# A four-layer transformer on one core: who normalises the MLP's rows, and how semaphores are cleared

## The reference, cut to what matters

```
for i in range(DEPTH):                      # 4
    y = layernorm(h, ln1_w[i], ln1_b[i])
    ...                                     # 8-head attention
    h = h + (o @ proj_w[i] + proj_b[i])
    y = layernorm(h, ln2_w[i], ln2_b[i])
    y = gelu(y @ fc1_w[i] + fc1_b[i])       # 128 -> 256
    h = h + (y @ fc2_w[i] + fc2_b[i])       # 256 -> 128
```

## Time and profile before

| | |
|---|---|
| time, median of 3 runs | 3908.1 us (3902.67 to 3911.08) |
| profiled execution, its own time | 3896.24 us |
| its span | 3894.5 us |
| granted TensorE clock, mean over the span | 0.95 of full speed |
| busy: PE, DVE, ACT, POOL | 3477.2, 2445.2, 1919.0, 2285.7 us |
| DVE L805, multiply by rstd | 128 times, 0.68 us |
| ACT L600, copy of `M2` | 128 times, 0.50 us |
| POOL L98, clears | 244 |

### The profile page before, as it was taken

How to read it: one execution, slowest core, us unless ns; L and a number is a source line. 1 busy time by engine, 2 the same in 40 slices (tenths; PEclk the granted TensorE clock), 3 DMA queues, 4 the chain that set the end, 5 groups by cost and what they waited for, 6 DMA issues and landing times. The chain is left out here.

```text
span 3894.5 us, 89214 instructions
## 1 busy us (share of the span) xinstructions
PE 3477.2 (89%) x30012; PEld 2650.4 (68%) x30012; DVE 2445.2 (63%) x6227; ACT 1919.0 (49%) x3500; POOL 2285.7 (59%) x2633
## 2 busy tenths in 40 slices
PE   6999999889999989999988999996997888989883
PEld 4567777667877767777666787775444666657662
DVE  2167776657777646777665777766995887743110
ACT  0156666436666535666643666653563433213331
POOL 0256663666665475666365666545994663463876
PEclk9999999989999989999998999998998999989986
DMA  6856663146776025666313667600111223232432
GB/s 220 246 103 129 128 130 74 20 76 122 132 128 131 11 57 99 131 128 129 74 20 74 128 129 131 129 2 26 35 32 29 63 63 45 54 82 45 70 58 29
DMA packets 456054, 342.05 MB, mean 88 GB/s; under 512 B 70659, under 2 KB 440171, under 8 KB 455595
## 3 DMA queue, kind: packets, MB, share of 16 engines
q1 hardware_dynamic: 404419, 275.69, 36.2%
q10 hardware_dynamic: 24224, 46.44, 3.7%
q0 software_dynamic: 27136, 16.42, 3.2%
HBM read 227.69 MB, written 109.29 MB: 87 GB/s over the span
## 5 line engine op out<-in xcount | busy, mean ns | idle before, releaser
L730 DVE TENSOR_REDUCE a_neg_max<-a_S 99x4 f32<-99x788 f32 x1024 | 1003.3, 980 | 491.1 <-PE a_S L319 486.8
L528 ACT ACTIVATE a_shared<-a_St 99x792 f32<-99x792 f32 (+1 forms) x1024 | 850.3, 830 | 614.2 <-PE a_St L336 602.7
L319 PE MATMUL a_S<-a_k_st,a_q_st 96*99 96x197 bf16 x4096 | 545.8, 256 | 47.0 <-DVE a_neg_max L730 46.8
L319 PEld LDWEIGHTS a_S<-a_k_st,a_q_st 96*99 96x99 bf16 x4096 | 394.4, 127 | 265.0 <-DVE a_neg_max L730 228.9
L336 PE MATMUL a_St<-a_q_st,a_k_st 99*99 99x198 bf16 (+1 forms) x4096 | 523.3, 250 | 43.0 <-DMA a_q_st<-a_max_rows 28.0
L355 PE MATMUL a_O<-a_shared,a_v_aug 99*32 99x198 f32 (+1 forms) x8192 | 461.8, 338 | 0.4
L336 PEld LDWEIGHTS a_St<-a_q_st,a_k_st 99*99 99x99 bf16 (+1 forms) x4096 | 385.8, 125 | 72.8 <-DMA a_q_st<-a_max_rows 32.8
L355 PEld LDWEIGHTS a_O<-a_shared,a_v_aug 99*32 99x32 f32 (+1 forms) x8192 | 246.2, 110 | 82.9 <-ACT a_shared L528 1.0
L659 POOL CAST a_parts<-a_q_k 128x792 bf16<-128x792 f32 x128 | 107.8, 843 | 311.1 <-issue 260.3
L673 POOL TENSOR_TENSOR h<-h,a_rows 99x512 f32<-99x512 f32 x128 | 163.2, 1275 | 212.4 <-DVE a_shared L805 212.4
L641 POOL CAST a_max_parts<-a_neg_max 99x32 bf16<-99x32 f32 x128 | 26.8, 209 | 440.7 <-DVE a_neg_max L730 440.7
(11 more groups left out here) (265 smaller groups left out, 7517.3 us busy)
## 6 DMA issues: line engine op xcount, KB each, us to landing
a_shared<-in_x ACTq DMA_DIRECT2D x64, 594.0 KB, 5.0
spill_q<-a_parts SPq DMA_DIRECT2D x384, 99.0 KB
spill_k<-a_parts SPq DMA_DIRECT2D x384, 99.0 KB
a_k_st<-spill_k SPq DMA_DIRECT2D x128, 297.0 KB
a_q_st<-spill_q SPq DMA_DIRECT2D x128, 297.0 KB
a_k_st<-spill_k SPq DMA_DIRECT2D x128, 198.0 KB
a_q_st<-spill_q SPq DMA_DIRECT2D x128, 198.0 KB
a_k_st<-spill_k SPq DMA_DIRECT2D x128, 99.0 KB
```

What stands on the lines that cost most here:

```text
L319: mm = nc.tensor.matmul(S[0:TC, j // 2, j % 2 * TB:j % 2 * TB + NTOK], q_st[p % 4][0:SPLIT, head, b * TB + c * TC:b * TB + (c + 1) * TC], ...
L528: nc.scalar.activation(probs[0:keys, u % 4, :].rearrange("p (x t) -> p x t", x=2), St[0:keys, :, 0:2 * TB], ACT.Exp).then_inc(s["probs"], 1)
L730: nc.vector.tensor_reduce(out.rearrange("p (x y) -> p x y", x=2), S[0:TC, :, 0:2 * TB].rearrange("p x (y t) -> p x y t", y=2)[:, :, :, 0:N ...
```

## The change

ACT, not DVE, multiplies the MLP's rows by rstd: four instructions of 128 columns in place of one of 512, for pair k+3 in turn k (before: pair k+2). DVE, not ACT, copies `M2` to `m_yT`, between the statistics and the addition to `h`. The statistics on DVE and the rstd on POOL are those of pair k+4, so one more filling turn, `mlp(l, -4)`, stands after step 30. POOL's bias stays with pair k+2. And `Sems.clear` issues one clear for each run of neighbouring semaphore numbers.

```diff
     def clear(self):
-        for s in self.all.values():
-            self.nc.gpsimd.sem_clear(s)
+        nums = sorted(s.num for s in self.all.values())
+        first = nums[0]
+        for a, b in zip(nums, nums[1:] + [None]):
+            if b != a + 1:
+                self.nc.gpsimd.sem_clear(range(first, a + 1))
+                first = b
         self.nc.all_engine_barrier()
...
                     step(l, PAIRS - 2)
+                    mlp(l, -4, -LEAD - 1)
                     mlp(l, -3, -LEAD - 1)
                     step(l, PAIRS - 1)
...                                                          # ACT, in mlp, behind the two Gelu
-                    if 0 <= k + 2 < PAIRS:
-                        n = at(l, k + 2)
-                        wait(act, s["m_turned"], n + 1)
-                        wait(act, s["m_fc1"], 2 * (n - 1))
-                        nc.scalar.activation(m_yT[n % 2], M2[:, 0:PW], ACT.Copy).then_inc(s["m_yT"], 1)
+                    if 0 <= k + 3 < PAIRS:
+                        n = at(l, k + 3)
+                        wait(act, s["m_rstd"], n + 1)
+                        wait(act, s["m_turned"], n - 1)
+                        for t in range(4):
+                            a = nc.scalar.activation(m_xn[n % 2][:, t, :], g.h[0:TC, (k + 3) * 4 + t, :], ACT.Copy,
+                                                     scale=m_rstd[n % 2][:, t, :])
+                        a.then_inc(s["m_xn"], 1)
...                                                          # POOL, in mlp, behind the bias
-                    if 0 <= k + 3 < PAIRS:
-                        n = at(l, k + 3)
+                    if 0 <= k + 4 < PAIRS:
+                        n = at(l, k + 4)
...                                                          # DVE, in mlp
-                    if 0 <= k + 2 < PAIRS:
-                        n = at(l, k + 2)
-                        wait(dve, s["m_rstd"], n + 1)
-                        wait(dve, s["m_turned"], n - 1)
-                        nc.vector.tensor_tensor(m_xn[n % 2], g.h[0:TC, (k + 2) * 4:(k + 3) * 4, :],
-                                                m_rstd[n % 2][:].to_broadcast([TC, 4, D]), ALU.mult).then_inc(s["m_xn"], 1)
-                    if 0 <= k + 3 < PAIRS:
-                        n = at(l, k + 3)
+                    if 0 <= k + 4 < PAIRS:
+                        n = at(l, k + 4)
...
+                    if 0 <= k + 2 < PAIRS:
+                        n = at(l, k + 2)
+                        wait(dve, s["m_turned"], n + 1)
+                        wait(dve, s["m_fc1"], 2 * (n - 1))
+                        nc.vector.tensor_copy(m_yT[n % 2], M2[:, 0:PW]).then_inc(s["m_yT"], 1)
```

More of the change, by code:

```diff
@@ L812, in mlp @@
                         for t in range(4):
-                            op = nc.vector.bn_stats(m_stats[q][:, t, :], g.h[0:TC, (k + 3) * 4 + t, :])
+                            op = nc.vector.bn_stats(m_stats[q][:, t, :], g.h[0:TC, (k + 4) * 4 + t, :])
                         op.then_inc(s["m_stats"], 1)
-                    if 0 <= k + 3 < PAIRS:
-                        n = at(l, k + 3)
-                        q = n % 2
                         wait(dve, s["m_stats"], n + 1)
```

## The result

The changed kernel takes 3861.64 us (median of 4 runs, 3849.33 to 3863.24), the kernel before 3908.72 (4 runs, 3902.67 to 3911.08). The ratio is 0.9873, with a 95% interval of 0.9851 to 0.9895: 47 us less where 28 were forecast. The direction was right, the size was not.

What follows compares the result with a forecast made beforehand. PE bounds plain MLP turns; turns with attention steps wait for POOL, and phases end in serial clears. Terms -16.1 (clears), -11.7 (POOL's chain), -1.6 (step -6), +1.2 (layers' ends) sum to -28.2 us: 3880 us, range 3868 to 3895.

Steps and rivals of the forecast that it cites:

- Clears: Phase ends: one range clear for each of six phases removes 238 clears of 67.7 ns, -16.1 us.
- The near end that I took: Phase ends: a range clear takes as long as a clear of a single number, giving -16.1 us.
- The rival of a range cleared at 67.7 ns a number: Phase ends: clears save nothing, only the MLP's -12 remain, 3896 us; chance 6%.
- Plain turn: MLP turns without an attention step: bound by PE at 3.42 us, nothing in the change reaches PE, 0 us.
- The rival of a late copy: Every MLP turn: DVE's copy to `m_yT` comes too late for PE, 3925 us; chance 3%.
- POOL's chain: Turns with attention steps -5 to -2: PE's wait for POOL's rows shrinks by 1.10 or 0.60 us, -11.7 us.
- Step -6: MLP turn with that attention step: of 1.00 us lost to late transposes 0.45 stay, three layers, -1.6 us.
- Layers' ends: End of each layer's attention: ACT's and DVE's new work adds about 0.3 us, four layers, +1.2 us.
- the term of the MLP: MLP of the layers: shorter PE waits in turns carrying attention steps, -11.7 and -1.6, together -13.3 us.
- a rival with 18%: Turns with attention steps: PE's clock follows the shorter waits, half of 15 us more gained, 3872 us; chance 18%.
- the edit should move profile and medians alike: Whole kernel: profiled 3896.24 becomes 3868, and the median 3908.1, 11.9 above it, becomes 3880 us.
- what is late next: Turns with steps -5 to -2: the same PE wait for POOL, shortened from 3.45 to 2.35 us, then ACT's copy.

Runs made afterwards that it cites:

- e1_clears: Kernel before with only the clears by ranges, MLP unchanged: 3850.21 us, ratio 0.9964 to the kernel before on the same chip.
- e6_one_input: Changed kernel plus three unused one-input `bn_stats` ahead of DVE's statistics: 3835.88 us, ratio 0.9942 to the kernel before.
- e5_two_inputs: Changed kernel plus an unused DVE multiplication with two SBUF inputs ahead of DVE's statistics: 3852.39 us, ratio 0.9994 to the kernel before.
- e2_mlp: Changed kernel with semaphores cleared one by one, so only the MLP part is new: 3841.74 us, ratio 0.9929 to the kernel before.
- e3_after: The changed kernel itself, run again on a second chip: 3824.11 us, ratio 0.9903 to the kernel before.
- e4_after_warm: Changed kernel plus nine unused identity products in PE's wait for POOL in steps -5 to -2: 3800.35 us, ratio 0.9836 to the kernel before.
- e7_before_warm: Kernel before plus twelve unused identity products in PE's wait for POOL in steps -5 to -2: 3837.28 us, ratio 0.9949 to the kernel before.
- e8_lead_only: Changed kernel, statistics still four turns ahead, but DVE multiplies the rows behind them and ACT copies: 3826.67 us, ratio 0.9922 to the kernel before.

## Why the prediction was wrong, point by point

**Clears: right.** Forecast -16.1; the profiled pair shows -15.7 (-4.5 and -11.2), and `e1_clears` alone -13 with an interval of 7 to 21. They are 67.6 ns each though a row shows 38: it was right to count from start to start. The MEMSET's idle time is 1.25 us, forecast about 1. The near end that I took, a range as quick as one number, is not quite what came: 236 clears are gone, not 238, and the eight that are left take 1.6 us together, some 5 ns for each further number of a range. The rival of a range cleared at 67.7 ns a number is refuted.

**Plain turn: right.** 3.42 us, last layer 105.21 before and after. ACT's four instructions 1.26 us (the measured value stood between the bounds 0.50 and 1.65; the estimate from the Trainium skill, ScalarE: Activation LUTs, What ACT_TABLE_LOAD costs, was put at 1.27, and its figures add up to 1.26), DVE's copy 0.57 (0.54). The rival of a late copy is refuted.

**POOL's chain: mechanism and waits right.** Statistics 0.59 earlier for 0.60; `xn` never long again; waits 27.6 us for 28. `e6_one_input` shows the first part by adding 0.6 back. That sharing SBUF is what the long `xn` was about is shown by the nine long ones, each just behind an L805, and by `e5_two_inputs`, where the delay moves to the other engine. The delay lies on the engine that comes second, which my text did not say. The Trainium skill (SBUF — State Buffer, SBUF: two separate sides) says that the two engines exclude each other for a whole instruction; the 1.20 us of DVE and the 0.56 of POOL's 4 columns agree. What the prediction took from the Trainium skill for one SBUF input held too (SBUF — State Buffer, Who interferes with whom: a VectorE instruction with at most one SBUF input does not contend with GpSimd). `xn` stays at 1.04 beside `bn_stats`.

**Step -6: right.** The two turns around it take 7.28 us instead of 7.84: 0.56 less for 0.55.

**Layers' ends: nearly nothing.** The +5.2 of the table is attention's scatter. From the start of the 24th exponential (L528 before, L533 after; eight belong to a step) ahead of a layer's first addition to `h` to that addition the least time is 47.39 to 47.40 us in the kernel before and in `e1_clears`, and 47.28 to 47.29 in the changed kernel, `e2_mlp` and `e3_after`. That is -0.1 us for each layer where +0.3 was forecast; the exponential of step 31 comes 0.4 later, as forecast in kind, and what follows it is 0.5 shorter.

**The failed step: the clock was put at nothing in the term of the MLP, -13.3 against -23.4.** The waits were sized right: PE's idle time in the first three layers' MLP fell by 13.6 us. What the sum left out is that PE itself got faster: its busy time there fell by 9.8 us for the same instructions. I had named this, but only as a rival with 18% (at half of 15 us). Step -5 of the first layer shows it as I worked it out (1.65 us of PE work for 1.7), and `e4_after_warm` shows that 24 us more of it were to be had. Where it came is luck: step -5 got it in one layer of three, step -2 in another, while step -4 ran at 0.83 or 0.84 in all of them.

**A second thing put at nothing, which mattered little in this result.** POOL's rstd one turn further ahead had no term. The trace of before had the wait that it removes, in one layer only, where it cost 1.2 us. `e7_before_warm` shows that 5.1 us a layer of it come out as soon as PE is fast. My text on what is late next looked along POOL's own chain alone.

**The carry from the profile to the medians failed as well, and it is the larger part of the miss.** I wrote that the edit should move profile and medians alike. The profiled pair moved by 33.8, the medians by 47.1: 13 of the 19 us that the forecast was short. The rest is 10 for the clock, less 4 by which the parts outside the MLP came out longer in the profiled pair than forecast. On the second chip the medians moved by 39, 11 more than forecast, which is about the clock's part alone. Why the profiled execution of before was 12 us quicker than the other runs stays open; the scatter of attention, which differs from one execution to the next, is a candidate and not shown.

## What to carry to other kernels

An engine that waits loses twice when its clock follows its gaps, so a cut of a wait can be worth more than its length (13.6 us of waits brought 9.8 of PE's own time with them here), and a wait that can't be cut may be filled with work that nobody needs: nine products a gap gave 24 us here. Before costing a slack at nothing, ask what it is once the engine that hid it is fast; here a lead of one more turn cost nothing in plain turns (the last layer's MLP stayed at 105.21 us). Where DVE and POOL both work on SBUF, give one of them an instruction that reads PSUM or a single SBUF input at that time.

## What the runs showed of the hardware

- A DVE instruction with two SBUF inputs and a POOL one delay each other, and the second one pays, even if it is short or comes only 8 to 17 ns later: POOL's 4 columns 0.56 for 0.20 us, its `xn` 1.54 for 1.04, its bias 1.72 for 1.27, DVE's 512 columns 1.20 and 1.75 for 0.68. Beside `bn_stats` POOL's `xn` stays at 1.04.
- The mean granted clock of the turn with step -5, by PE's wait for `xn` in it: 0.84, 0.70, 0.84 at 3.45 us (kernel before); 0.83 three times at 2.89 (`e6_one_input`); 1.00 twice and 0.69 once at 2.66 (`e8_lead_only`); 1.00 four times and 0.82 five times at 2.30. The wait's length alone does not tell the clock.
- 244 semaphore clears take 67.6 ns each on POOL, though a row shows 38. A clear of a range took 48 ns for 2 numbers, 243 for 38 and 418 for 72.
- The phases after the layers took 1189.2 us in the first profile of the changed kernel and 1139.4 in `e3_after`, the same program on another chip: ratios within a chip are what can be compared.
